# Four edits to the first attention stage of a four-stage Trainium2 kernel: V's low half by TensorE and ScalarE, the layer norm's last step on ScalarE, the bias on GpSimd, the output tile by blocks

## The chip, the cores and the metric

The kernel runs on one core of one Trainium2 chip. The metric is device time in microseconds (us) of one launch, the median of several runs. The engines are named as the profile names them: PE (TensorE, matmuls), PEld (TensorE's weight loads), DVE (VectorE), ACT (ScalarE), POOL (GpSimd) and SP (SyncE, which issues most of the DMAs). Each engine works through its own list in order, and semaphores tie the lists together.

## The reference

Four layers follow one another on an input of 8 batches of 512 tokens of width 128: attention with relative positions (16 heads of size 64), a top-2 mixture of experts, a second attention, and a mixture of experts with capacity. Behind each stands a residual sum and a layer norm without learned scale. The change touches the first layer alone. Cut to it:

```python
def _layernorm(x, axis=-1, eps=1e-05):
    m = jnp.mean(x, axis=axis, keepdims=True)
    v = jnp.var(x, axis=axis, keepdims=True)
    return (x - m) / jnp.sqrt(v + eps)
...
        w = qkv * (3.0 * x * h * n) ** (-0.25)
        q, k, v = jnp.einsum('bsx,xAnh->Abnsh', input, w)
        q = q + q_bias[:, None, :]
        a = jnp.einsum('bnqh,bnkh->bnqk', q, k) * h ** (-0.5)
...
        a = a + relative_causal(pos_scores)
        mask = jnp.tril(jnp.ones((s, s), dtype=bool))
        a = jax.nn.softmax(jnp.where(mask, a, NEG_INF), axis=-1)
        o = jnp.einsum('bnqk,bnkh->bqnh', a, v).reshape(b, s, n * h)
        fan_in, fan_out = out_kernel.shape
        out = o @ (out_kernel * (fan_in * fan_out) ** (-0.25)) + out_bias
        return out
```

The first layer's result is the layer norm of `input + out`.

## The kernel before

The first attention is `rel_attention_phase`. It takes the profile's stretch from about 35 us to 763 us. Its unit of work is a **pair** of heads of one batch: 8 pairs (`PAIRS`) by 8 batches (`B`), numbered `n`, with `p` the pair in its batch and `k` the parity of a double buffer. `schedule` writes the same loop on every engine: it calls `body(n, t, b, p, k)` once for each pair. The order of `body` on an engine is the order of its list. Nothing reorders it.

Products run in float16 halves: each operand is split into a high half and the rest, and three matmuls take the place of one. Who makes the halves:

- **POOL**, `split_k` and `split_q`: four splits in a pair (K and Q of head 0, then of head 1), each an affine select that writes the high half (L705) and a subtraction for the low half (L708). They are made for pair n+1 while pair n is worked on. `split_k(0, n+1)` waits for ACT's `k_copy`. PE's `scores(h, n+1)` (L483 to L486) wait for the splits of head h.
- **The probabilities**: ACT's `exps` (L565) and `high` (L574), then DVE's `low` (L618), which reads the 128x1280 probabilities and their high half, both in SBUF. SP transposes both halves by DMA.
- **V**: PE's `project_v` writes V to the PSUM tile `v_ps`. ACT's `v_high` (L580) copies it to the float16 tile `v_h`. DVE's `v_low` (L637) writes the rest, `v_l`.

DVE's `body` for a pair is: `maxima` of head 0 (L606), `reciprocals` and `low` of head 1 of the pair before, `q_evac` (L624), `reciprocals` (L614), `normalise` of the pair two before (L632), `low` of head 0, `maxima` of head 1, `q_evac` of the next pair, `v_low`. ACT's is: three groups of `exps` with `k_copy` (L586) between, `high`, `v_high`, then `exps` and `high` of head 1. PE's is: scores of head 0, projections of K and Q of head 0 of the next pair and V of this one, `weighted_values` (L502) of the pair two before, scores of head 1, projection of Q of head 1, and `project_out` (L519) of the pair two before, which uses the tile `o32` as weights. `o32` has the query index outside and the block index c inside, so that a block's weights are every fourth float32.

Once in a batch more is done. At the last pair (`wrap`) DVE adds the output bias to this batch's rows of `m.x` (`add_bias`, L642) and applies the layer norm of the batch before (`batch_norm`, the helper at L123: subtract the mean, multiply by the inverse deviation, four instructions). At the third pair (p = 2) DVE sums output and residual and takes the statistics of the batch before, and POOL makes the inverse deviation (`layer_norm_gpsimd`, L136 and L137).

## Time and profile before

| | us |
|---|---|
| median of three runs | 1621.62 |
| lowest and highest run | 1618.57, 1624.36 |
| the profiled execution | 1622.89 |
| its span | 1621.2 |
| PE busy in the span | 1395.3 (86%) |
| DVE busy | 1300.4 (80%) |
| ACT busy | 944.1 (58%) |
| POOL busy | 886.5 (55%) |

Shares of busy time run over all four stages. In the first stage DVE, PE and POOL each show nine or eight tenths in most slices, so that a share alone doesn't tell which one sets the pace. What tells it is the idle time in front of an instruction and the engine that ended it. A row of the view in order of time gives the start in us from the span's start, the duration in us, the engine, the line, the operation, the tiles written and read, and in brackets the idle time before it with what ended it.

### The profile page before, as it was taken

The page shows a single profiled execution, that of the slowest core. Times are in us where ns is not written, and L with a number is a line of the kernel's source. Part 1 is how long each engine was busy: PE and PEld are TensorE (multiplying, and loading weights), DVE is VectorE, ACT ScalarE, POOL GpSimd, SP SyncE. Part 2 cuts the span into 40 slices and gives each one's busy share as a digit, 9 for nine tenths or more (in the row PEclk, how much of TensorE's full clock was granted, in tenths as well). Part 3 has the DMA queues.
Part 4 walks back from the last instruction along what each step waited for, and adds up shares of the span by engine and source line. Part 5 has one row for each costly group of instructions (what it writes and reads, how often), then busy time and mean ns, then how long its engine had stood idle before and what let it go on. Part 6 is the DMA issues. An engine that isn't in the chain of part 4 may idle for free. (4 is left out here: it accounts for less than half of the span.)

```text
span 1621.2 us, 36711 instructions
## 1 busy us (share of the span) xinstructions
PE 1395.3 (86%) x11495; PEld 838.3 (52%) x11495; DVE 1300.4 (80%) x2722; ACT 944.1 (58%) x1857; POOL 886.5 (55%) x943
## 2 busy tenths in 40 slices
PE   4799999999999999995798987489899899997936
PEld 3477767676776767674465664123333332332316
DVE  3689899999899999996688888377787887887834
ACT  2577767776767777673244443156666666665631
POOL 2678878888888878785355555211221231231635
PEclk9799999999999999997699999599999999999978
DMA  5667766665666656663000000421011111101001
GB/s 161 123 144 156 142 147 142 145 150 137 152 140 151 145 138 150 143 146 85 1 1 0 0 0 16 138 50 34 28 39 33 32 33 31 39 27 32 26 8 33
DMA packets 401552, 133.51 MB, mean 82 GB/s; under 512 B 362155, under 2 KB 389792, under 8 KB 401376
## 3 DMA queue, kind: packets, MB, share of 16 engines
q1 hardware_dynamic: 398144, 128.41, 33.7%
q10 hardware_dynamic: 1824, 3.15, 0.6%
q0 software_dynamic: 1536, 1.34, 0.3%
q8 instruction: 26, 0.43, 0.1%
q14 instruction: 22, 0.18, 0.0%
HBM read 37.14 MB, written 13.15 MB: 31 GB/s over the span
## 5 line engine op out<-in xcount | busy, mean ns | idle before, releaser
L565 ACT ACTIVATE prob<-score_ps,nmax 128x512 f32<-128x512 f32 (+3 forms) x512 | 264.1, 524 | 194.5 <-DVE nmax L606 193.9
L1577 DVE TENSOR_REDUCE a_nm<-a_s 128x1 f16<-128x512 f32 x512 | 324.5, 687 | 53.1 <-PE a_s L1349 52.1
L1503 ACT ACTIVATE a_pt<-a_st 128x1024 f32<-128x1024 f32 x256 | 260.5, 1021 | 122.0 <-PE a_st L1367 118.8
L1349 PE MATMUL a_s<-a_kop,a_qop 128*128 128x512 f16 x512 | 198.2, 388 | 59.1 <-DVE a_nm L1577 42.3
L606 DVE TENSOR_REDUCE nmax<-score_ps 128x1 f32<-128x512 f32 (+3 forms) x512 | 219.3, 480 | 19.6 <-PE score_ps L486 17.2
L618 DVE SCALAR_TENSOR_TENSOR p<-prob,p 128x1280 f16<-128x1280 f32 x128 | 224.6, 1755 | 3.4 <-ACT p L574 3.3
L708 POOL TENSOR_TENSOR q_l<-q,q_h 128x512 f16<-128x512 f32 x130 | 202.3, 1556 | 10.8
L483 PE MATMUL score_ps<-k_h,q_h 128*128 128x512 f16 (+3 forms) x512 | 158.2, 309 | 37.2 <-POOL q_l L708 31.2
L574 ACT ACTIVATE p<-prob 128x1280 f16<-128x1280 f32 x128 | 162.6, 1270 | 8.4
L708 POOL TENSOR_TENSOR k_l<-k,k_h 64x512 f16<-64x512 f32 x130 | 157.8, 1214 | 10.8
L902 ACT ACTIVATE hid<-fps,b_cols 128x512 f32<-128x512 f32 x130 | 86.4, 687 | 126.6 <-PE fps L862 126.6
L485 PE MATMUL score_ps<-k_h,q_l 128*128 128x512 f16 (+3 forms) x512 | 157.2, 307 | 0.0
L484 PE MATMUL score_ps<-k_l,q_h 128*128 128x512 f16 (+3 forms) x512 | 157.1, 307 | 0.0
L998 POOL TENSOR_TENSOR hid_l<-hid,hid_h 128x512 f16<-128x512 f32 x65 | 97.1, 1494 | 106.4 <-DVE hid_h L966 106.4
L1367 PE MATMUL a_st<-a_qop,a_kop 128*128 128x512 f16 x512 | 152.2, 380 | 0.2
L1349 PEld LDWEIGHTS a_s<-a_kop,a_qop 128*128 128x128 f16 x512 | 50.5, 99 | 184.7 <-DVE a_nm L1577 151.6
L705 POOL TENSOR_SCALAR_AFFINE_SELECT q_h<-q 128x512 f16<-128x512 f32 x130 | 122.9, 945 | 39.7 <-POOL k_l L708 34.4
L1380 PE MATMUL a_pv<-a_pt,a_vaug 128*32 128x512 f32 x1024 | 137.0, 607 | 0.7 <-ACT a_pt L1503 0.7
L519 PEld LDWEIGHTS out_ps<-wo,o 128*128 128x128 f32 x512 | 124.3, 327 | 18.6 <-DVE o L632 12.1
L519 PE MATMUL out_ps<-wo,o 128*128 128x128 f32 (+1 forms) x512 | 125.2, 389 | 9.2 <-DVE o L632 9.2
L705 POOL TENSOR_SCALAR_AFFINE_SELECT k_h<-k 64x512 f16<-64x512 f32 x130 | 84.0, 646 | 84.6 <-ACT k L586 68.5
L502 PE MATMUL pv_ps<-pt,v_h 128*64 128x256 f16 (+1 forms) x1536 | 119.1, 259 | 2.2 <-DMA pt<-p 2.2
(328 smaller groups left out, 3216.6 us busy)
## 6 DMA issues: line engine op xcount, KB each, us to landing
r_bc<-r_parts SPq DMA_DIRECT2D x128, 128.0 KB, 2.9
a_qop<-q_parts SPq DMA_DIRECT2D x32, 128.0 KB
a_kop<-k_parts SPq DMA_DIRECT2D x128, 24.0 KB
x_tok<-in_L_attn_input_dram SPq DMA_DIRECT2D x4, 512.0 KB, 12.4
pt<-p SPq DMA_TRANSPOSE x128, 4.1
r_parts<-rsum SPq DMA_DIRECT2D x128, 2.0 KB, 2.1
e_w<-in_L_ffn_w_dram SPq DMA_DIRECT2D x1, 2048.0 KB, 8.8
q_parts<-a_q_h SPq DMA_DIRECT2D x16, 128.0 KB
```

What stands on the lines that cost most here:

```text
L483: nc.tensor.matmul(o, q_h[h][:, qs], m.k_h[h][:, 0:w], start=True, stop=False)
L485: nc.tensor.matmul(o, q_l[h][:, qs], m.k_h[h][:, 0:w], start=False, stop=False)
L519: mm = nc.tensor.matmul(out_ps[:, cs], o32[:, :, c], w, start=False, stop=(end and c == QC - 1), skip_group_check=True)
L565: ins = nc.scalar.activation(prob[h][:, P_OFF[c]:P_OFF[c] + w], score_ps[u][:, col:col + w], ACT.Exp, bias=nmax[h][:, c:c + 1], accum_out= ...
L574: nc.scalar.activation(p16[h][k][:, 0, :], prob[h][:, :], ACT.Copy, scale=P_SCALE).then_inc(p_hi[h], 1)
L606: ins = nc.vector.tensor_reduce(nmax[h][:, c:c + 1], score_ps[u][:, col:col + P * (c + 1)], AX.X, ALU.max, negate=True)
L618: nc.vector.scalar_tensor_tensor(p16[h][k][:, 1, :], prob[h][:, :], P_SCALE, p16[h][k][:, 0, :], ALU.mult, ALU.subtract).then_inc(p_lo[h], 1)
L705: nc.gpsimd.affine_select(out=hi, in_=src, compare_op=ALU.is_ge, fill=0.0, base=0, pattern=[[1, S]], channel_multiplier=0).then_inc(pool_s ...
L708: return nc.gpsimd.tensor_tensor(lo, src, hi, ALU.subtract)
L1349: nc.tensor.matmul(s_ps[k][:, :], qop[:, g, c * P:(c + 1) * P], kop[:, hh, g, :], start=True, stop=True).then_inc(s_mm[k], 1)
L1503: nc.scalar.activation(pt[kc % 2][r][:, :, :], st_ps[r][:, :, :], ACT.Exp, scale=1.0 / SC).then_inc(exp_done[r], 1)
L1577: nc.vector.tensor_reduce(nm[g % 2][:, c, hh:hh + 1], s_ps[c % 2][:, :], AX.X, ALU.max, negate=True).then_inc(max_done[c % 2], 1)
```

## The change

Four things move, and some semaphores with them.

1. **V's low half.** V is kept in PSUM without its scale, and its halves are made of V/32. ACT copies V/32 to `v_h`. A new PE matmul (`take_high`, behind the scores of head 1) adds `v_h` times minus 32 to `v_ps`, through the new tile `take` (a scaled identity), which leaves V less its high half. A new ACT copy (`v_low`, behind `v_high`) takes that to `v_l`. DVE's `v_low` goes. The missing scale stands in the factor of `batch_sum`.
2. **The layer norm's last step** becomes an ACT instruction with a bias and a scale from pointers, four for each batch, behind `high` of head 1 of the last pair. POOL makes the minus mean and its product with the inverse deviation (`norm_terms`): four small instructions in place of two.
3. **The output bias** is added by POOL, four instructions of 128x128, behind the splits of the second pair (p = 1).
4. **`o32`** is laid out by blocks: PE's weights are 128 neighbouring float32, and DVE writes with a step of 128 elements.

Also: the semaphores `r_done` and `f0_loaded` go, SP's `store_r` waits for `p_lo` in place of `r_done` (in its list the same semaphore value has been waited for just ahead), PE waits once at the start for `take`, and the later stages wait for one counter of all weight loads.

```diff
...
 P_SCALE = 1024.0
+V_SCALE = 1.0 / 32
...
         r_bc = [sb(f"r_bc{k}", [P, S], F32) for k in range(2)]
-        o32 = sb("o32", [P, P, QC], F32)
+        o32 = sb("o32", [P, S], F32)
...
         rstd = sb("ln_rstd", [P, QC], F32)
+        take = sb("take_away", [P, P], F16)
+        nmean, shift = sb("ln_nmean", [P, QC], F32), sb("ln_shift", [P, QC], F32)
...
         k_mm, k_out, k_split = sem("k_mm"), sem("k_out"), pair("k_split")
-        v_mm, v_hi, v_lo = sem("v_mm"), sem("v_hi"), sem("v_lo")
+        v_mm, v_hi, v_rest, v_lo = sem("v_mm"), sem("v_hi"), sem("v_rest"), sem("v_lo")
...
         s_mm, max_done, exp_done = pair("s_mm"), pair("max_done"), pair("exp_done")
-        p_hi, p_lo, r_done = pair("p_hi"), pair("p_lo"), pair("r_done")
+        p_hi, p_lo = pair("p_hi"), pair("p_lo")
...
-                sp.wait_ge(r_done[h], n + 1)
+                sp.wait_ge(p_lo[h], n + 1)
...
                     o = v_ps[:, c * P:(c + 1) * P]
-                    nc.tensor.matmul(o, x_hi, w_hi, start=True, stop=False)
-                    nc.tensor.matmul(o, x_hi, w_lo, start=False, stop=False)
-                    mm = nc.tensor.matmul(o, x_lo, w_hi, start=False, stop=True)
+                    nc.tensor.matmul(o, x_hi, w_hi, start=(c == 0), stop=False, skip_group_check=True)
+                    nc.tensor.matmul(o, x_hi, w_lo, start=False, stop=False, skip_group_check=True)
+                    mm = nc.tensor.matmul(o, x_lo, w_hi, start=False, stop=False, skip_group_check=True)
...
+            def take_high(n, k):
...
+                pe.wait_ge(v_hi, n + 1)
+                nc.tensor.matmul(v_ps[:, :], take[:, :], v_h[k][:, :, :].rearrange("p c n -> p (c n)"), start=False, stop=True,
+                                 skip_group_check=True).then_inc(v_rest, 1)
...
                     cs = slice(c * P, (c + 1) * P)
-                    mm = nc.tensor.matmul(out_ps[:, cs], o32[:, :, c], w, start=False, stop=(end and c == QC - 1), skip_group_check=True)
+                    mm = nc.tensor.matmul(out_ps[:, cs], o32[:, cs], w, start=False, stop=(end and c == QC - 1), skip_group_check=True)
...
             def first_front():
+                pe.wait_ge(bias_in, 1)
...
                 scores(1, n)
+                take_high(n, k)
...
                 nc.scalar.activation(v_h[k][:, :, :].rearrange("p c n -> p (c n)"), v_ps[:, :], ACT.Copy,
-                                     scale=W_SCALE).then_inc(v_hi, 1)
+                                     scale=V_SCALE).then_inc(v_hi, 1)
...
+            def v_low(n, k):
+                act.wait_ge(v_rest, n + 1)
+                nc.scalar.activation(v_l[k][:, :, :].rearrange("p c n -> p (c n)"), v_ps[:, :], ACT.Copy,
+                                     scale=V_SCALE).then_inc(v_lo, 1)
...
+            def batch_norm(b):
+                act.wait_ge(m.rstd_ready, b + 1)
+                for c in range(QC):
+                    ins = nc.scalar.activation(m_flat(m.x)[:, ds(b * S + c * D, D)], y[:, c, :], ACT.Identity,
+                                               bias=shift[:, c:c + 1], scale=rstd[:, c:c + 1])
+                ins.then_inc(ln_dve, 1)
...
                 v_high(n, k)
+                v_low(n, k)
...
                 high(1, n, t, k)
+                if at(p, PAIRS - 1) and not at(b, 0):
+                    batch_norm(b - 1)
...
             nc.scalar.preload_act_table(ACT.Exp)
-            schedule(act, lambda: k_copy(0), body, lambda: None)
+            schedule(act, lambda: k_copy(0), body, lambda: batch_norm(B - 1))
...
                     dve.wait_ge(r_stored, 32 * (n - 1))
-                nc.vector.reciprocal(rsum[h][k][:, :], sums[h][:, :]).then_inc(r_done[h], 1)
+                nc.vector.reciprocal(rsum[h][k][:, :], sums[h][:, :])
...
                     dve.wait_ge(out_mm, n)
-                nc.vector.tensor_tensor(o32[:, :, :], pv_ps[:, :].rearrange("p (c q) -> p q c", q=P),
+                nc.vector.tensor_tensor(o32[:, :].rearrange("p (c q) -> p q c", q=P), pv_ps[:, :].rearrange("p (c q) -> p q c", q=P),
...
-
-            def v_low(n, k):
-                dve.wait_ge(v_hi, n + 1)
-                nc.vector.scalar_tensor_tensor(v_l[k][:, :, :].rearrange("p c n -> p (c n)"), v_ps[:, :], W_SCALE,
-                                               v_h[k][:, :, :].rearrange("p c n -> p (c n)"), ALU.mult, ALU.subtract).then_inc(v_lo, 1)
...
-
-            def add_bias(b):
-                xb = m_flat(m.x)[:, ds(b * S, S)].rearrange("p (c d) -> p c d", d=D)
-                nc.vector.tensor_tensor(xb, xb, m.bo_bc[:, :].unsqueeze(1).to_broadcast([P, QC, D]), ALU.add).then_inc(bias_in, 1)
...
                 dve.wait_ge(out_mm, PAIRS * (b + 1))
-                dve.wait_ge(bias_in, b + 1)
+                dve.wait_ge(bias_in, b + 2)
...
                 dve.wait_ge(ln_dve, b + 1)
-                nc.vector.scalar_tensor_tensor(y[:, :, :].rearrange("p c d -> p (c d)"), out_ps[:, :], O_SCALE / P_SCALE,
+                nc.vector.scalar_tensor_tensor(y[:, :, :].rearrange("p c d -> p (c d)"), out_ps[:, :], O_SCALE * W_SCALE / (P_SCALE * V_SCALE),
...
-            def batch_norm(b):
-                layer_norm_apply(nc, dve, m, b, y, mv, rstd,
-                                 m_flat(m.x)[:, ds(b * S, S)].rearrange("p (c d) -> p c d", d=D)).then_inc(ln_dve, 1)
...
                 wrap = at(p, PAIRS - 1)
-                behind = wrap and not at(b, 0)
...
                 q_evac(1, n + 1, pw)
-                v_low(n, k)
-                if wrap:
-                    add_bias(b)
-                if behind:
-                    batch_norm(b - 1)
...
                 vector_gate(nc, m).then_inc(ln_dve, 1)
+                nc.vector.tensor_scalar(take[:, :], m.ident[:, :], -1.0 / V_SCALE, None, ALU.mult).then_inc(bias_in, 1)
...
                 batch_stats(B - 1)
-                batch_norm(B - 1)
...
                 split_q(1, n + 1)
+                if at(p, 1):
+                    add_bias(b)
                 if at(p, 2) and not at(b, 0):
-                    layer_norm_gpsimd(nc, pool, m, b - 1, mv, ve, rstd)
+                    norm_terms(b - 1)
+            def add_bias(b):
+                for c in range(QC):
+                    xc = m_flat(m.x)[:, ds(b * S + c * D, D)]
+                    ins = nc.gpsimd.tensor_tensor(xc, xc, m.bo_bc[:, :], ALU.add)
+                ins.then_inc(bias_in, 1)
+            def norm_terms(b):
+                steps = Steps(pool, m.ln_pool, 2 * b)
+                pool.wait_ge(m.var_ready, b + 1)
+                nc.gpsimd.tensor_tensor(nmean[:, :], mv[:, :, 0], m.minus[:, :], ALU.mult)
+                steps.step(nc.gpsimd.tensor_tensor(ve[:, :], mv[:, :, 1], m.eps[:, :], ALU.add))
+                steps.step(nc.gpsimd.tensor_tensor(rstd[:, :], ve[:, :], m.mhalf[:, :], ALU.pow))
+                nc.gpsimd.tensor_tensor(shift[:, :], nmean[:, :], rstd[:, :], ALU.mult).then_inc(m.rstd_ready, 1)
```

What stands in a row on DVE at the end of a batch's last pair and in front of the next batch, before:

```order
L632 TENSOR_TENSOR o<-pv_ps,r_bc 128x512
L618 SCALAR_TENSOR_TENSOR p_01<-prob,p_01 128x1280
L606 TENSOR_REDUCE nmax<-score_ps 128x1 x4
L624 SCALAR_TENSOR_TENSOR q_1<-q_ps,q_bias,q_mult 128x512
L637 SCALAR_TENSOR_TENSOR v_l<-v_ps,v_h 128x512
L642 ISA
L642 TENSOR_TENSOR x_tok<-x_tok,bo_bc 128x512
L123 TENSOR_SCALAR x_tok<-ln_y,ln_mv,ln_rstd 128x128
```

And there now:

```order
L640 RECIPROCAL rsum<-sums 128x4
L658 TENSOR_TENSOR o<-pv_ps,r_bc 128x128x4
L644 SCALAR_TENSOR_TENSOR p_01<-prob,p_01 128x1280
L632 TENSOR_REDUCE nmax<-score_ps 128x1 x4
L650 SCALAR_TENSOR_TENSOR q_1<-q_ps,q_bias,q_mult 128x512
L357 REGISTER_ALU
L357 COMPARE_AND_BRANCH
L640 RECIPROCAL rsum<-sums 128x4
```

`v_low`, the bias and the four steps of the layer norm (the first of them is the last row of the first piece) are gone from DVE.

On POOL, the end of a batch's second pair (in all batches but the first), before:

```order
L708 TENSOR_TENSOR k_l<-k,k_h 64x512
L705 AFFINE_SELECT q_h<-q_1 128x512
L707 REGISTER_ALU
L708 TENSOR_TENSOR q_l<-q_1,q_h 128x512
L719 REGISTER_ALU
L720 REGISTER_ALU
```

Now:

```order
L715 TENSOR_TENSOR k_l<-k,k_h 64x512
L712 AFFINE_SELECT q_h<-q_1 128x512
L714 REGISTER_ALU
L715 TENSOR_TENSOR q_l<-q_1,q_h 128x512
L750 ISA
L750 TENSOR_TENSOR x_tok<-x_tok,bo_bc 128x128
L750 ISA
L750 TENSOR_TENSOR x_tok<-x_tok,bo_bc 128x128
```

The row pairs at L750 come four times, and the next pair's splits start behind them.

On ACT, from `v_high` of a batch's last pair on, now (`p_11` and `prob` are head 1's probabilities):

```order
L590 REGISTER_ALU
L591 ACTIVATE v_h<-v_ps 128x512
L596 ACTIVATE v_l<-v_ps 128x512
L576 ACTIVATE prob,sums<-score_ps,nmax 128x512
L576 ACTIVATE prob,sums<-score_ps,nmax 128x384
L576 ACTIVATE prob,sums<-score_ps,nmax 128x128
L576 ACTIVATE prob,sums<-score_ps,nmax 128x256
L585 ACTIVATE p_11<-prob 128x1280
L602 ISA
L602 ACTIVATE x_tok<-ln_y,ln_shift,ln_rstd 128x128
L602 ISA
```

The second copy of V (L596) is new behind the first (L591), and the layer norm (L602, four times) stands ahead of the next batch's first exponentials.

## Rows read from the trace of the kernel before

**Rows 1.** Busy time by engine between K copies: stretch, length, PE, PEld, DVE, ACT, POOL.

```profile
473.01:486.70 13.69, 12.93 (x143) 9.74 (x140) 12.95 (x22) 7.80 (x22) 9.72 (x9) 1.00 0.49 116
486.70:496.32 9.62, 8.11 (x59) 5.53 (x57) 9.32 (x17) 7.69 (x22) 7.73 (x8) 1.00 0.67 158
...
549.64:560.01 10.37, 10.04 (x99) 7.55 (x97) 9.57 (x17) 7.69 (x22) 9.20 (x9) 1.00 0.67 151
sum 87.00, PE 82.07 PEld 61.00 DVE 81.25 ACT 61.96 POOL 73.68; mean PE 10.26 PEld 7.62 DVE 10.16 ACT 7.75 POOL 9.21
```

**Rows 2.** POOL in order of time, one ordinary pair.

```profile
466.38 1.56 POOL L705 TENSOR_SCALAR_AFFINE_SELECT q_h<-q 128x512 f16<-128x512 f32 x1 [0.26 <-POOL k_l L708]
468.02 1.16 POOL L708 TENSOR_TENSOR q_l<-q,q_h 128x512 f16<-128x512 f32 x1
...
472.14 2.43 POOL L708 TENSOR_TENSOR q_l<-q,q_h 128x512 f16<-128x512 f32 x1
```

**Rows 3.** DVE in order of time, the same pair.

```profile
464.67 0.69 DVE L632 TENSOR_TENSOR o<-pv_ps,r_bc 128x512 f32<-128x512 f32 x1 [0.67 <-PE pv_ps L502]
465.28 2.19 DVE L618 SCALAR_TENSOR_TENSOR p<-prob,p 128x1280 f16<-128x1280 f32 x1
...
469.64 0.68 DVE L637 SCALAR_TENSOR_TENSOR v_l<-v_ps,v_h 128x512 f16<-128x512 f32 x1
470.24 1.85 DVE L606 TENSOR_REDUCE nmax<-score_ps 128x1 f32<-128x512 f32 x4
...
472.09 1.46 DVE L618 SCALAR_TENSOR_TENSOR p<-prob,p 128x1280 f16<-128x1280 f32 x1
```

**Rows 4.** PE in order of time: output projection, next scores; transposes in the second stage.

```profile
477.52 1.92 PE L519 MATMUL out_ps<-wo,o 128*128 128x128 f32 x8
479.77 0.39 PE L483 MATMUL score_ps<-k_h,q_h 128*128 128x512 f16 x1 [0.33 <-POOL q_l L708]
...
766.82 1.97 PE L826 MATMUL fps<-ident,x_tok 128*128 128x128 f32 x8 [2.49 <-DVE wg_l L918]
```

**Rows 5.** DVE in order of time, the last pair of a batch.

```profile
480.69 1.50 DVE L642 TENSOR_TENSOR x_tok<-x_tok,bo_bc 128x512 f32 x1
482.11 2.39 DVE L123 TENSOR_SCALAR x_tok<-ln_y,ln_mv,ln_rstd 128x128 f32 x4
484.41 1.67 DVE L606 TENSOR_REDUCE nmax<-score_ps 128x1 f32<-128x512 f32 x4
```

**Rows 6.** ACT in order of time, the same place.

```profile
478.55 0.69 ACT L565 ACTIVATE prob<-score_ps,nmax 128x512 f32<-128x512 f32 x1 [2.61 <-DVE nmax L606]
...
480.73 1.27 ACT L574 ACTIVATE p<-prob 128x1280 f16<-128x1280 f32 x1
485.13 0.69 ACT L565 ACTIVATE prob<-score_ps,nmax 128x512 f32<-128x512 f32 x1 [3.13 <-DVE nmax L606]
...
486.36 0.36 ACT L565 ACTIVATE prob<-score_ps,nmax 128x128 f32<-128x128 f32 x1
486.70 0.60 ACT L586 ACTIVATE k<-k_ps 128x512 f32<-128x512 f32 x1
```

**Rows 7.** POOL in order of time: behind the wrap, then the next batch's third pair.

```profile
487.58 0.60 POOL L705 TENSOR_SCALAR_AFFINE_SELECT k_h<-k 64x512 f16<-64x512 f32 x1 [3.69 <-ACT k L586]
...
507.56 1.23 POOL L705 TENSOR_SCALAR_AFFINE_SELECT k_h<-k 64x512 f16<-64x512 f32 x1 [0.59 <-ACT k L586]
...
517.42 1.45 POOL L136 TENSOR_TENSOR ln_ve<-ln_mv,ln_eps 128x4 f32<-128x4 f32 x1
```

**Rows 8.** POOL groups over the whole span: count, busy us, mean ns.

```profile
L1699 POOL TENSOR_TENSOR a_vaug<-a_v,a_bv 128x128 f32<-128x128 f32 x32 | 14.4, 454 | 184.0 <-PE a_pv L1380 129.7 <-DVE a_v L1552 54.3
L1743 POOL TENSOR_TENSOR a_scale<-a_mv,a_rstd 128x4 f32<-128x4 f32 x8 | 1.6, 202 | 0.6
```

**Rows 9.** Weight load groups over the whole span: weights in steps of four, weights side by side.

```profile
L519 PEld LDWEIGHTS out_ps<-wo,o 128*128 128x128 f32 x512 | 124.3, 327 | 18.6 <-DVE o L632 12.1
L826 PEld LDWEIGHTS fps<-ident,x_tok 128*128 128x128 f32 x32 | 5.9, 218 | 7.8 <-issue 5.2 <-DVE wg_l L918 2.6
```

More of the change, by code:

```diff
@@ L133, in layer_norm_gpsimd @@
 def layer_norm_gpsimd(nc, pool, m, n, mv, ve, rstd):
-    steps = Steps(pool, m.ln_pool, n)
+    steps = Steps(pool, m.ln_pool, n + B)
     pool.wait_ge(m.var_ready, n + 1)
@@ L271, in _ @@
             nc.gpsimd.memset(m.eps[:, :], LN_EPS)
+            nc.gpsimd.memset(m.minus[:, :], -1.0)
             nc.gpsimd.memset(m.b2_blocks[:, :], 0.0)
@@ L364, in _ @@
         def _(sp):
-            load = lambda dst, src: sp.dma_start(dst, src).then_inc(m.f0_loaded, 16)
+            load = lambda dst, src: sp.dma_start(dst, src).then_inc(m.a_loaded, 16)
             load(m.w1_raw[:, :, :], io["L0_ffn_W1"].rearrange("e d f -> d e f"))
@@ L373, in _ @@
             load(m.iota8[:, :], io["c_iota8"])
-            loads = 0
+            loads = 10 * 16
             def load(dst, src, scattered=False):
@@ L442, in _ @@
             schedule(sp, lambda: None, body, last)
-            sp.wait_ge(m.f0_loaded, m.F0_LOADS)
             sp.wait_ge(m.a_loaded, loads)
@@ L734, in body @@
                 split_q(1, n + 1)
+                if at(p, 1):
+                    add_bias(b)
                 if at(p, 2) and not at(b, 0):
-                    layer_norm_gpsimd(nc, pool, m, b - 1, mv, ve, rstd)
+                    norm_terms(b - 1)
[11 more added lines that the diff above has]
+                nc.gpsimd.tensor_tensor(shift[:, :], nmean[:, :], rstd[:, :], ALU.mult).then_inc(m.rstd_ready, 1)
             def last():
-                layer_norm_gpsimd(nc, pool, m, B - 1, mv, ve, rstd)
+                norm_terms(B - 1)
             schedule(pool, lambda: front(0), body, last)
@@ L828, in _ @@
                 if t == 0:
-                    pe.wait_ge(m.f0_loaded, m.F0_LOADS)
+                    pe.wait_ge(m.a_loaded, m.A_LOADS)
                     nc.tensor.transpose(hid_ps[0][:, 0:E0 * FC], m.b1_rows[:, :], m.ident[0:E0 * FC, 0:E0 * FC]).then_inc(b1_mm, 1)
@@ L914, in _ @@
             steps = Steps(dve, dsteps)
-            dve.wait_ge(m.f0_loaded, m.F0_LOADS)
+            dve.wait_ge(m.a_loaded, m.A_LOADS)
             nc.vector.tensor_copy(wg_h[:, :], m.wg_raw[:, :]).then_inc(wg_split, 1)
@@ L998, in low @@
                 nc.gpsimd.tensor_tensor(hid_l[k][1][:, :], hid32[k][1][:, :], hid_h[k][1][:, :], ALU.subtract).then_inc(h_lo[1], 1)
-            pool.wait_ge(m.f0_loaded, m.F0_LOADS)
+            pool.wait_ge(m.a_loaded, m.A_LOADS)
             for hi, raw in ((w1_h, m.w1_raw), (w2_h, m.w2_raw)):
@@ L1961, in build @@
         m.eps = sb("ln_eps", [P, QC], F32)
+        m.minus = sb("ln_minus", [P, QC], F32)
         m.gate_v = sb("gate_v", [P, 1], F32)
@@ L1974, in build @@
         m.iota8 = sb("iota8", [P, E0], F32)
-        m.f0_loaded = ctx.enter_context(nc.semaphore("f0_loaded"))
-        m.F0_LOADS = 10 * 16
         m.a_w = sb("a_w_raw", [P, 5, D], F32)
```

## The prediction, made before the changed kernel was run

> **What bounds the kernel now.** All four edits lie in the first attention, so I read that stage alone, first by stretches. Busy time between two K copies of ACT gives the length of each pair: eight pairs, one batch, take 87.0 us, an ordinary one 10.37, the last of a batch 13.69, the one behind it 9.62 [rows 1]. Then I read each engine in order of time, for what it waits for.
>
> In an ordinary pair POOL waits for nobody. Its four splits follow one another with 0.26 us or less between, and they are longer than their work: an affine select (0.60 in rows 7) once takes 1.56, a subtraction of 1.16 once takes 2.43 [rows 2]. Both times DVE's `low` is running: `low` of head 0 is asked for at 465.28, waits until the K subtraction ends at 466.12 (0.26 us before 466.38), and holds the select that starts at 466.38; `low` of head 1 starts at 472.09, 0.05 us ahead of the subtraction at 472.14 [rows 2, 3]. So POOL's splits plus 0.95 and 1.27 us of such stalls make up 10.4 us, and that is the pair. PE is nearly as full: its output projection ends at 479.44 and the next scores start at 479.77, where POOL's low half of Q releases them [rows 4]. DVE has 0.67 us in front of `normalise` [rows 3], ACT 2.61 us in front of its exponentials of head 1 [rows 6]. **POOL sets an ordinary pair.** The Trainium skill, "SBUF — State Buffer", section "SBUF: two separate sides", says the same of the port that VectorE and GpSimd share: it is locked for a whole instruction by a GpSimd operation or by a VectorE one with two SBUF inputs. By that rule `v_low`, with one input in PSUM, takes nothing from POOL, and the trace agrees: it has its 0.68 us in rows 3.
>
> At a batch's end the bound is another one. DVE does the bias (1.42 us to the next start) and the layer norm (2.30) before it comes to the maxima at 484.41 [rows 5]; ACT waits 3.13 us for them, and the K copy comes at 486.70 [rows 6]; POOL waits 3.69 us for that copy [rows 7]. **There DVE sets the time.**
>
> **V's low half.** DVE loses 0.60 us (469.64 to 470.24) in each of 64 pairs [rows 3]. The maxima behind it read scores that PE started 0.14 us after POOL's subtraction ended at 469.18 [rows 2, 4]; the first unit takes PE some 0.92, which gives 470.24. The maxima would start when they start now, so I count 0. If POOL were no bound, the whole 0.60 would count. PE gains one matmul with 512 columns, whose kind takes 0.39 in rows 4 and less to the next start. The 0.33 us in front of the scores covers it [rows 4]. Its wait for `v_h` holds up only the Q projection and the output projection; the copy is done before the scores of head 1 end. ACT gains a copy of 0.60 (as the K copy [rows 6]), which waits for that matmul. The hole of 2.61 us holds the wait and the copy: scores of head 1 end near 476.9, the matmul near 477.3, the copy near 477.9, and the exponentials start at 478.55. I take 0; the bounds are -0.6 and +0.4 for each pair.
>
> **The wrap.** Bias and layer norm leave DVE, so the maxima start near 480.7 instead of 484.41. ACT then ends `high` of head 1 at 481.9 (start 480.73 and 1.18 to the next) and does the layer norm itself. No row shows this instruction. The nearest is the exponential of 128 columns, 0.36, or 0.34 to the next start [rows 6]; its input is in PSUM and it has one pointer. I take 0.38 each, 1.5 for four, bounds 1.2 and 1.9. The next exponentials then start at 483.4 instead of 485.13: **-1.7 for a wrap**, and not the 3.7 that DVE loses. POOL's hole of 3.69 mostly closes: `low` of head 1 now comes near 482.5, stalls the subtraction there by 1.27, and POOL ends near 485.0, still ahead of the K copy. Six wraps make -10.2. The last one has no maxima and exponentials behind it: `low` stands right behind the layer norm, which by rows 5 is the time 484.41, and now waits only for its own high half (481.9) and the end of a split, some 0.3 later: -2.2. The first has the bias alone, and there the same stall of POOL takes the gain back: -0.2. Sum -12.6.
>
> **Bias on POOL.** Four instructions of 128x128: 0.45 each [rows 8], with an address instruction between that the trace shows as 0.07 or so elsewhere, or 0.41 each if they overlap as neighbours do: 1.65 to 2.1. They are put behind the splits of the second pair. POOL has a hole there, 0.59 in front of the split at 507.56, but that split ends only at 508.79, since `low` holds it until 508.2 [rows 7]; the hole hides nothing. Behind the four, `low` of head 0 now meets the K splits instead of the subtraction of Q, so the scores come 1.7 to 2.4 later. POOL carries this to the next batch's wrap, for it has no other hole.
>
> **The small terms.** `norm_terms` has two instructions of 0.20 more, one behind a wait: +0.45 in each batch [rows 8]. The first of the four takes the stall that makes 1.45 of the first one now [rows 7]. With the bias I count 2.6 for a batch (bounds 1.6 and 3.4), seven batches, **+18.2**. In the first batch POOL has holes of several us and the term is 0. At the end of the stage the norm is on the path: 0.3 for POOL, 0.4 for ACT against DVE; and 0.3 for the wait for `take` at the start: +1.0.
>
> **`o32` by blocks.** A weight load takes 327 ns in steps of four and 218 side by side [rows 9]. Yet eight output matmuls take 1.92 and eight with neighbouring weights 1.97 [rows 4]: the loads run under the matmuls, and the gain is 0 to 0.1 for a pair, where PE has 0.33 to spare: 0. DVE now writes at a step of 512 bytes, which no row shows. Bounds: 0 (reading PSUM at that step costs nothing seen: 0.69 for 512 columns in rows 3) and, by the 109 ns that 128 weights lose in rows 9, four times that, 0.44. In an ordinary pair `normalise` may end 0.8 us later before `low` is later, since `low` waits for the K subtraction anyway [rows 2, 3]. I take 0. The Trainium skill, same page, section on the DMA port swizzle, speaks against this edit: it says that accesses which each cross to a new 16-byte line pay a penalty. By the weight loads the trace agrees; by the same price DVE would lose 0.44, the second rival's term.
>
> **Sum.** -12.6 + 18.2 + 1.0 = +6.6 us against the profiled execution's 1622.9 (span 1621.2, 1.7 around it). The median is 1.3 below it, so the forecast is 1621.6 + 6.6 = **1628 us**, 0.4% slower.
>
> **The rivals.**
> 1. *POOL takes the new work in its holes.* If the bias falls where POOL waits for the K copy, or the order of the locks turns once in a batch so that a stall of 1.27 goes, a batch costs 1.3 less: -9, 1619. For it speaks that the margin is 0.05 us [rows 2, 3]; against it that POOL has no hole in six pairs of eight. If both happen, 2.6 a batch go and the wraps alone count: 1610. 25% and 8%.
> 2. *The strided write is on DVE's path.* At 0.44 or more, `low` of head 0 in the pairs where DVE has no slack (the first and third of a batch) starts behind the next POOL instruction and loses up to 1.2 more: 1 us for each of 15 pairs, +13 with the new stalls, 1641. It decides from 0.8 us of extra write in an ordinary pair: then all 64 lose. 17%.
> 3. *The order of locks turns in every pair.* If PE's new matmul delays the scores by more than 0.05 us, the subtraction goes ahead of `low`, POOL gains about 0.5 a pair: -28, 1595. Against it: PE has 0.33 to spare [rows 4]. 5%.
> 4. *The edit does nothing:* `o32` is such a case already, in the sum with 0. That the DVE instructions go is seen in the order of the lists.
>
> **How the numbers follow.** Forecast 1628, its own spread 1621 to 1635: 45%. Rival 1: 33%, rival 2: 17%, rival 3: 5%. A difference of 0.3%, 4.9 us, is about what a measurement of this kernel can tell from none: below 1616.7 is faster, above 1626.5 slower. Faster: rival 3, the 8% and a little of the rest, 0.22. Slower: rival 2 and 60% of the forecast, 0.44. Same: 0.34. The range leaves out rival 3 and the tails: 1608 to 1642.
>
> **What would show it.** Right: ordinary pairs stay at 10.4, DVE idle before the maxima of head 0 where `v_low` was; the wrap falls to about 12; POOL's hole there falls below 1; the third pair of a batch grows by 2 us or more. Wrong: ordinary pairs shorter than 10.2 (DVE was the bound, or the locks turned), `normalise` longer than 0.7 us, ACT's norm instruction above 0.5 us, or the third pair unchanged, which would say that POOL had room.

## The result: 0.7% slower

| | before | changed |
|---|---|---|
| median, us (five runs each) | 1624.31 | 1635.96 |
| lowest and highest | 1618.57, 1624.56 | 1632.54, 1638.00 |
| the profiled execution | 1622.89 | 1635.96 |
| its span | 1621.2 | 1634.2 |

The ratio of changed to before is 1.0073, with a 95% interval of 1.0059 to 1.0088. The forecast was 1628 us, some 6.6 us slower; the spans differ by 13.0. The direction was right, the size was half of it.

Where the 13.0 us come from, by the starts of ACT's K copies: the first one comes 1.2 us later (38.0 for 36.9), from there to the last it is 11.5 us more (708.6 for 697.1), and from the last to the end of the program 0.4 more. In that last part the first stage ends 1.2 us earlier, and the stages that weren't changed take 1.6 more. That 1.6 can't be put down to the edits: over all traces of this document those stages take between 857.7 and 860.9 us.

The same batch as in [rows 1], now: busy time of each engine between K copies of ACT. Columns: stretch, length, busy time of PE, PEld, DVE, ACT and POOL with the count of instructions, granted TensorE clock, DMA share, GB/s.

```profile
480.60:492.58 11.98, 10.99 (x131) 8.25 (x130) 10.05 (x17) 9.82 (x27) 10.80 (x9) 1.00 0.70 143
492.58:502.17 9.59, 8.17 (x74) 5.49 (x70) 7.86 (x14) 8.25 (x23) 7.74 (x8) 1.00 0.75 146
502.17:512.52 10.35, 9.46 (x102) 6.82 (x99) 9.12 (x17) 8.27 (x23) 9.18 (x9) 1.00 0.76 158
512.52:524.40 11.88, 9.61 (x101) 6.87 (x99) 11.26 (x25) 8.29 (x23) 10.87 (x13) 1.00 0.65 133
524.40:537.15 12.75, 10.04 (x90) 6.84 (x87) 8.70 (x16) 8.62 (x24) 11.37 (x13) 0.87 0.65 134
537.15:549.00 11.85, 10.92 (x113) 7.65 (x111) 10.12 (x16) 8.40 (x22) 8.03 (x8) 1.00 0.61 120
549.00:558.85 9.85, 9.37 (x101) 6.79 (x98) 8.61 (x16) 8.29 (x24) 7.96 (x8) 1.00 0.80 163
558.85:569.23 10.38, 9.41 (x100) 6.77 (x98) 9.07 (x16) 8.30 (x24) 9.21 (x9) 1.00 0.77 152
```

Before, the eight pairs took 13.69, 9.62, 10.37, 11.09, 10.65, 10.76, 10.45 and 10.37. The wrap (first row) has lost 1.7 us. The fourth to sixth have gained 0.8, 2.1 and 1.1, the seventh lost 0.6. In the fifth row the clock is 0.87, in all others 1.00. This is so in every batch from the second to the eighth (once a 0.99 stands behind the 0.87). Before, the clock is below 1.00 in one pair of the second, third and fifth batch (0.83 to 0.86), and in none of the other four.

By batch, the lengths are:

| batch | 1 | 2 | 3 | 4 | 5 | 6 | 7 | 8 |
|---|---|---|---|---|---|---|---|---|
| before | 88.7 | 85.4 | 87.4 | 87.0 | 87.6 | 87.0 | 87.0 | 87.0 |
| changed | 88.3 | 88.2 | 88.7 | 88.7 | 88.7 | 88.7 | 88.8 | 88.7 |

POOL of the changed kernel in order of time: the bias (L750), and the first and last of the layer norm's four small instructions.

```profile
512.76 2.95 POOL L750 TENSOR_TENSOR x_tok<-x_tok,bo_bc 128x128 f32 x4
...
525.90 0.20 POOL L757 TENSOR_TENSOR ln_nmean<-ln_mv,ln_minus 128x4 f32<-128x4 f32 x1
...
527.43 1.50 POOL L760 TENSOR_TENSOR ln_shift<-ln_nmean,ln_rstd 128x4 f32<-128x4 f32 x1
```

The bias takes 2.91 us to the next start. DVE's `low` runs from 512.11 to 514.15 meanwhile and holds the port. The four small ones take 2.98 us up to the start of the select that follows, where two took 2.50 before; the last of them stands under a `low` again (1.50 for 0.20).

PE of the changed kernel, from the output projection (L528) of the third pair on, L492 the first scores of a pair, L456 to L458 the projection of K:

```profile
517.37 1.05 PE L528 MATMUL out_ps<-wo,o 128*128 128x128 f32 x8
520.69 0.39 PE L492 MATMUL score_ps<-k_h,q_h 128*128 128x512 f16 x1 [2.27 <-POOL q_l L715]
520.92 0.38 PE L493 MATMUL score_ps<-k_l,q_h 128*128 128x512 f16 x1
...
532.88 0.39 PE L492 MATMUL score_ps<-k_h,q_h 128*128 128x512 f16 x1 [2.71 <-POOL q_l L715]
...
536.05 0.63 PE L457 MATMUL k_ps<-xt_h,w_l 128*128 x1
536.48 0.63 PE L458 MATMUL k_ps<-xt_l,w_h 128*128 x1
```

Two things stand here that the prediction doesn't have. The eight output matmuls (the trace shows two for each of the four calls) take 1.05 us in place of the 1.92 of [rows 4]. And PE waits 2.27 and then 2.71 us for POOL, where it waited 0.46 (for ACT) and 1.01 before. Soon behind the second wait the clock falls from the higher to the lower of its levels: from 533.75 to about 537.2 matmuls of 512 columns come 0.43 us apart (536.05 and 536.48) in place of 0.22 or so (520.69 and 520.92). The K copy waits for that. It comes 4.27 us behind the first scores (537.15 and 532.88); in e4_filler below, where the clock is held, it comes 3.39 behind them, so that the fall makes it 0.9 us late.

### The profile page after: what moved, and what is told of

Same layout as the page of the kernel before. It is cut to its first block and busy times, and to the rows that moved or that the text cites. A ratio compares the mean times of both kernels' runs of the same rounds, so it can differ in the third digit from the quotient of the medians.

```text
span 1634.2 us, 36942 instructions
## 1 busy us (share of the span) xinstructions
PE 1357.1 (83%) x11559; PEld 791.3 (48%) x11559; DVE 1252.3 (77%) x2619; ACT 993.2 (61%) x1953; POOL 907.8 (56%) x992
## 3 DMA queue, kind: packets, MB, share of 16 engines
q1 hardware_dynamic: 398144, 128.41, 36.9%
## 5 line engine op out<-in xcount | busy, mean ns | idle before, releaser
L492 PE MATMUL score_ps<-k_h,q_h 128*128 128x512 f16 (+3 forms) x512 | 158.0, 309 | 82.9 <-POOL q_l L715 73.5
L644 DVE SCALAR_TENSOR_TENSOR p<-prob,p 128x1280 f16<-128x1280 f32 x128 | 215.0, 1680 | 3.9 <-ACT p L585 3.4
L715 POOL TENSOR_TENSOR q_l<-q,q_h 128x512 f16<-128x512 f32 x130 | 201.5, 1550 | 10.8
L715 POOL TENSOR_TENSOR k_l<-k,k_h 64x512 f16<-64x512 f32 x130 | 152.4, 1172 | 10.8
L712 POOL TENSOR_SCALAR_AFFINE_SELECT k_h<-k 64x512 f16<-64x512 f32 x130 | 85.4, 657 | 74.6 <-ACT k L609 58.4
L1723 POOL TENSOR_TENSOR a_vaug<-a_v,a_bv 128x128 f32<-128x128 f32 x32 | 14.4, 453 | 184.1 <-PE a_pv L1404 129.8
L495 PE MATMUL score_ps<-causal,ident_bf 128*128 128x128 bf16 x512 | 114.8, 224 | 0.0
```

The costliest lines, as they stand in the source:

```text
L492: nc.tensor.matmul(o, q_h[h][:, qs], m.k_h[h][:, 0:w], start=True, stop=False)
L644: nc.vector.scalar_tensor_tensor(p16[h][k][:, 1, :], prob[h][:, :], P_SCALE, p16[h][k][:, 0, :], ALU.mult, ALU.subtract).then_inc(p_lo[h], 1)
L712: nc.gpsimd.affine_select(out=hi, in_=src, compare_op=ALU.is_ge, fill=0.0, base=0, pattern=[[1, S]], channel_multiplier=0).then_inc(pool_s ...
L715: return nc.gpsimd.tensor_tensor(lo, src, hi, ALU.subtract)
```

## Experiments

All times below are medians of 6 to 12 runs beside 23 to 35 runs of the kernel before on the same chip; before stood at 1622.9, 1621.5 and 1622.4 us in the three groups. A batch's length is taken from the K copies of the profiled execution. A steady batch is one from the third to the eighth.

### One edit undone

The changed kernel with the bias on DVE, the layer norm on DVE, or the old `o32`:

```diff
 # e1_bias_dve: POOL's add_bias goes; DVE, behind q_evac(1, n + 1, pw):
+                if wrap:
+                    add_bias(b)
 # e2_norm_dve: ACT's batch_norm and POOL's norm_terms go; DVE, same place:
+                if wrap and not at(b, 0):
+                    batch_norm(b - 1)
 # e3_o32_old; the weights of project_out and the write of normalise follow
-        o32 = sb("o32", [P, S], F32)
+        o32 = sb("o32", [P, P, QC], F32)
```

> The changed kernel with one edit undone: the output bias is added by DVE behind the last pair's second q_evac again, in one instruction. Theory A (the bias on POOL is what costs: the three pairs behind it grew by 0.8, 2.1 and 1.0 us against the kernel before, and one got 0.6 shorter): a batch falls from 88.7 to 85.7 to 86.5 us, seven batches give back 15 to 21 us, time 1615 to 1621, below the kernel before (ratio 0.995). The wrap stays within 0.5 us of 11.98, since 1.42 us of bias on DVE lie beside ACT's 1.6 us of layer norm. Theory B (the wider write of o32 or the new copies of V cost in every pair): nothing changes, 1632 to 1638.

Measured: 1620.91 us, ratio 0.999 (0.9978 to 1.0002). Steady batches take 86.0 to 87.6, the wrap 11.98. That is theory A's time at its upper edge: the ratio falls from 1.0073 to 0.999, which is some 13 us and less than the 15 to 21 expected. The bias on DVE costs the wrap nothing beside ACT's layer norm. It doesn't follow that the bias alone made the kernel slow, for the third run below gives back nearly as much without touching it.

> The changed kernel with the layer norm's last step on DVE again, and POOL with its two instructions for the inverse deviation in place of four. Theory A: at the wrap DVE does 2.3 us more and ACT 1.6 less, so the wrap grows by 0.2 to 0.7 us; POOL loses 0.2 to 1.5 us a batch in the fourth pair (its last small instruction stands under a lock of low for 1.5). Sum -1 to +0.3 a batch: 1628 to 1638, ratio 1.003 to 1.009. Rival: the layer norm on ACT is worth its whole 1.7 us a wrap, 1645 or more.

Measured: 1627.04, ratio 1.0026 (1.0016 to 1.0037), better than both expected. The wrap is 11.77, so ACT's layer norm brings nothing there once the bias is off DVE. Without the two small instructions PE waits 2.1 in place of 2.7 us in the fourth pair, and the clock falls there in four of the last six batches: those take 87.9 to 88.2, the other two 86.5 and 86.7.

> The changed kernel with o32 laid out as before. normalise falls from 1.06 to 0.69 us, eight output matmuls rise from 1.05 to 1.92 us. Theory A (POOL sets ordinary pairs): ordinary pairs stay at 10.37, since PE keeps some 0.1 us ahead of the scores; the stretches in which PE waits long for scores are shorter by 0 to 0.9: 1633 to 1638. Theory B (the wide write stands on DVE's path): -13, 1621 to 1625. Theory C (the faster projection is what keeps PE off the path, with V's extra matmul): PE's 1.92 and 0.22 more fill its slack of 0.33, pairs grow by 0.1 to 0.3, 1640 to 1650.

Measured: 1623.97, ratio 1.0005 (0.9993 to 1.0017). This is theory B's number, some 11 us back by the ratios, where theory A had 3 at most. Yet ordinary pairs stay at 10.37, so B's mechanism, a cost in every pair, is wrong. The clock still falls in five of the last seven batches. DVE, POOL and the stretches around such a fall, with the old layout (L658 `normalise`, L644 `low`, L715 the subtraction of Q):

```profile
429.80:442.70 12.90, 11.34 (x92) 7.99 (x90) 8.11 (x16) 8.50 (x23) 11.10 (x13) 0.87 0.63 132
442.70:453.20 10.50, 10.50 (x104) 7.95 (x103) 8.45 (x16) 8.43 (x23) 8.17 (x8) 1.00 0.70 138
```

```profile
445.49 0.69 DVE L658 TENSOR_TENSOR o<-pv_ps,r_bc 128x512 f32<-128x512 f32 x1 [1.10 <-PE pv_ps L511]
446.09 1.55 DVE L644 SCALAR_TENSOR_TENSOR p<-prob,p 128x1280 f16<-128x1280 f32 x1
```

```profile
446.38 2.27 POOL L715 TENSOR_TENSOR q_l<-q,q_h 128x512 f16<-128x512 f32 x1
```

And the same place in the changed kernel:

```profile
540.35 1.06 DVE L658 TENSOR_TENSOR o<-pv_ps,r_bc 128x512 f32<-128x512 f32 x1 [1.32 <-PE pv_ps L511]
541.25 2.19 DVE L644 SCALAR_TENSOR_TENSOR p<-prob,p 128x1280 f16<-128x1280 f32 x1
```

```profile
540.95 1.16 POOL L715 TENSOR_TENSOR q_l<-q,q_h 128x512 f16<-128x512 f32 x1
```

With the old layout `low` comes 0.29 us ahead of the subtraction and the pair takes 10.50. With the new one `normalise` is 0.3 us longer, `low` comes 0.30 us behind the subtraction, takes 2.19, and the pair takes 11.85. The write is half of this shift: `normalise` also starts 0.29 us nearer to the subtraction (0.60 ahead for 0.89). So the layout helps to turn an order of locks here, in the pair behind a fall of the clock. In f2_o32_only below the write alone turns it.

### The clock held up

```diff
                     project_out(n - 2, ...)
+                if at(p, 2) or not isinstance(p, int):
+                    for _ in range(8 if at(p, 2) else 4):
+                        nc.tensor.matmul(out_ps[:, :], m.zeros[:, 0:P], m.zeros[:, :], start=False, stop=False, ...)
```

> The changed kernel with work added to PE alone: zeros are added to out_ps, eight matmuls of 512 columns behind the output projection of the third pair of each batch and four in each of the four pairs behind it (0.22 us each, 1.8 and 0.9 us, into stretches in which PE waits 2.3, 2.7 and 0.9 us). Theory C2 (half of the extra cost is TensorE's clock: behind two waits of 2.3 and 2.7 us the granted clock of one pair is 0.87 and its matmuls take 0.63 in place of 0.38 for some 3.5 us): with PE kept busy the clock stays at 1.00, that pair and the next lose 1 to 2.5 us, seven batches 7 to 17 us: 1619 to 1629. Theory A alone (POOL sets the pace there too): 1633 to 1638. If the added matmuls cost by themselves: above 1640.

Measured: 1628.29, ratio 1.0038 (1.0025 to 1.0051). Work was added, and the time fell: by the ratios some 6 us, by the profiled spans 6.8 (1627.4 for 1634.2). The second row is the stretch that had 0.87:

```profile
508.10:519.98 11.88, 11.34 (x109) 7.56 (x107) 11.26 (x25) 8.30 (x23) 10.87 (x13) 1.00 0.65 132
519.98:531.84 11.86, 10.01 (x101) 6.83 (x98) 8.38 (x16) 8.53 (x24) 10.69 (x13) 1.00 0.71 144
531.84:542.60 10.76, 10.65 (x111) 7.46 (x109) 9.35 (x16) 8.40 (x24) 9.59 (x9) 1.00 0.69 133
542.60:553.05 10.45, 10.42 (x108) 7.23 (x104) 9.21 (x16) 8.30 (x24) 9.28 (x9) 1.00 0.74 151
```

From the third batch on the clock is 1.00 in all pairs; 12.75 + 11.85 + 9.85 have become 11.86 + 10.76 + 10.45, and the batch 87.3 (88.1 in the third). POOL's and DVE's lists are those of the changed kernel. So of the 1.7 us that most batches grew by, the fall of the clock with what follows from it makes 1.4. PE still waits 1.85 us in the stretch that had 0.87.

### One edit alone

Each is the changed kernel with the other three undone.

> Only the first edit is left of the four: V's low half by PE and ACT. Bias and layer norm are on DVE at the wrap, o32 is laid out as before. Theory A (POOL sets an ordinary pair): ordinary pairs stay at 10.37 to 10.45; the wrap, which DVE sets, gets 0.6 us shorter (13.69 to 13.1), 7 wraps make -4: 1616 to 1622, ratio 0.996 to 1.000. Rival: PE's extra matmul takes the slack of 0.33 us in front of the scores and turns the order of the locks, then pairs change by 0.1 or more, that is 6 us or more either way.

Measured: 1619.35, ratio 0.9989 (0.9980 to 0.9998). Ordinary pairs are unchanged to 0.1 us, the wrap is 13.35, 0.33 shorter, and a batch 86.6.

> Only the layer norm's last step is moved to ACT, with its four small instructions on POOL. DVE leaves 2.3 us at the wrap, ACT's exponentials start behind its layer norm: the wrap falls from 13.69 to 12.0 to 12.3. POOL's two further instructions cost 0.2 to 1.2 us a batch. Sum -1.6 to -0.3 a batch: 1611 to 1620, ratio 0.993 to 0.998. If the layer norm on ACT is worth nothing, 1622 or more.

Measured: 1619.02, ratio 0.9982 (0.9970 to 0.9993). The wrap is 11.98, a steady batch 85.9 to 86.8; in three of the last six the clock falls in one pair.

> Only the bias is moved to POOL, in its place behind the splits of the second pair. The wrap gets 1.4 us shorter (12.3), the pairs behind the four instructions together 2.2 to 3.3 longer: +0.8 to +1.9 a batch, 1628 to 1636. Theory D: PE's waits there are shorter than in the changed kernel (its output projection takes 1.92 us), so that the granted clock stays at 1.00 in most batches and the lower end is right; if the clock falls here as well, the upper.

Measured: 1632.95, ratio 1.0065 (1.0053 to 1.0077), the upper end. The wrap is 13.02, only 0.7 shorter. In five of the last six batches the clock falls in two pairs, to 0.83 and 0.86, and they take 88.5 to 88.9; in the last it doesn't fall, and that takes 87.9. So the bias's own cost is 0.9 us a batch, 1.6 in the pairs behind the wrap less 0.7 at the wrap.

> Only the layout of o32 is changed, all else as in the kernel before. Theory D (the layout costs nothing by itself, but lengthens PE's waits and so lets the clock fall where POOL is late): without the bias on POOL PE's longest waits of a batch are near 2 us, and ordinary pairs stay at 10.37; with no pair below a clock of 1.00 in the steady batches 1620 to 1626, with one such pair a batch 1630 to 1634. Theory B (normalise, 0.37 us longer, stands on DVE's path in every pair): 64 times 0.3, 1640 or more.

Measured: 1633.58, ratio 1.0069 (1.0049 to 1.0088). The layout alone costs as much as all four edits. From the third batch on each takes 88.8 or 88.9, and the clock is 0.87 in the fourth stretch. Theory D gave the number. What it left out is where a part of PE's wait comes from. The third pair, DVE (L635 `normalise`, L621 `low`), then POOL (L710) and PE:

```profile
515.27 1.03 DVE L635 TENSOR_TENSOR o<-pv_ps,r_bc 128x512 f32<-128x512 f32 x1
516.15 2.45 DVE L621 SCALAR_TENSOR_TENSOR p<-prob,p 128x1280 f16<-128x1280 f32 x1
```

```profile
516.10 1.16 POOL L710 TENSOR_TENSOR q_l<-q,q_h 128x512 f16<-128x512 f32 x1
```

```profile
520.07 0.39 PE L486 MATMUL score_ps<-k_h,q_h 128*128 128x512 f16 x1 [2.55 <-ACT prob L568]
```

In the kernel before, the same two engines in the same place:

```profile
510.16 0.66 DVE L632 TENSOR_TENSOR o<-pv_ps,r_bc 128x512 f32<-128x512 f32 x1
510.74 1.50 DVE L618 SCALAR_TENSOR_TENSOR p<-prob,p 128x1280 f16<-128x1280 f32 x1
```

```profile
510.98 2.27 POOL L708 TENSOR_TENSOR q_l<-q,q_h 128x512 f16<-128x512 f32 x1
```

Before, `low` is asked for 0.24 us ahead of the subtraction. Now `normalise` is 0.30 longer, `low` comes 0.05 behind it and takes 2.45 for 1.50. The maxima are 1.25 us later, ACT and the scores with them. PE has done its output projection 0.84 us sooner. The two add up to the 2.09 us by which PE's wait has grown, from 0.46 to 2.55, and no run parts them. Then the clock falls: matmuls take the longer time from 520.5 to 523.9.

The same filler as above in this kernel:

> The layout of o32 changed alone, as one run before (88.8 us a batch, one pair at a granted clock of 0.87), and zeros added to out_ps by PE behind the output projection: eight matmuls of 0.22 us in the third pair, four in each of the next four. Theory D (of the 1.8 us a batch that the layout costs, one part is that low of head 0 comes behind POOL's subtraction in the third pair, 0.95 us, and the other the clock that falls behind PE's wait of 2.55 us): the clock stays at 1.00, a batch falls to 87.2 to 87.9 us, 1624 to 1629, between the two kernels. If the wide write costs by itself and not the clock: 1632 to 1636.

Measured: 1631.59, ratio 1.0051 (1.0035 to 1.0067), slower than expected. The clock is held where the filler stands, but in four batches it falls two pairs earlier, where there is none. First the third pair of the fifth batch, where the clock is held, and the pair behind it; then a stretch where it falls:

```profile
423.69:436.04 12.35, 11.49 (x110) 7.42 (x106) 12.31 (x26) 7.70 (x22) 10.20 (x11) 1.00 0.65 130
436.04:445.98 9.94, 9.94 (x103) 7.05 (x101) 9.21 (x17) 7.70 (x22) 8.93 (x9) 1.00 0.80 158
```

```profile
490.83:501.49 10.66, 8.32 (x50) 4.76 (x49) 9.34 (x17) 7.93 (x23) 8.02 (x8) 0.84 0.70 141
```

The fifth and eighth batch have the clock at 1.00 throughout: both take 87.2, for 88.8 without filler and 87.0 in the kernel before. The other four of the steady ones take 87.5 to 88.4. That some 1.6 of the 1.8 us hang on the clock is read from two batches, then, and not from the median.

In these two batches the order of locks is turned all the same (L638 `normalise`, L624 `low`, L713 the subtraction):

```profile
427.13 1.03 DVE L638 TENSOR_TENSOR o<-pv_ps,r_bc 128x512 f32<-128x512 f32 x1
428.01 2.45 DVE L624 SCALAR_TENSOR_TENSOR p<-prob,p 128x1280 f16<-128x1280 f32 x1
```

```profile
427.95 1.16 POOL L713 TENSOR_TENSOR q_l<-q,q_h 128x512 f16<-128x512 f32 x1
```

The pair takes 12.35 for 11.09, but the next two take 9.94 and 10.37 for 10.65 and 10.76, so that all but 0.2 us comes back. With the clock held, the turned order costs next to nothing.

### Versions built on this

The bias needs no time of POOL, and of DVE only once, in the first pair, to make its two halves: PE opens `out_ps` with a matmul of zeros anyway.

```diff
 # g1_bias_pe: the changed kernel, POOL's add_bias goes, PE's open_output:
-                nc.tensor.matmul(out_ps[:, :], m.zeros[:, 0:P], m.zeros[:, :], start=True, stop=False, ...)
+                for i, t in enumerate((bo_h, bo_l)):
+                    nc.tensor.matmul(out_ps[:, :], ones[:, :], t[:, :, :].rearrange(...), start=(i == 0), stop=False, ...)
 # g2_norm_early: g1, and in ACT's body the layer norm stands here
                 v_high(n, k)
+                if at(p, PAIRS - 1) and not at(b, 0):
+                    batch_norm(b - 1)
                 v_low(n, k)
 # g3_best: g2 with o32 as in the kernel before
```

> The changed kernel without a bias on POOL or DVE: PE's matmul of zeros that opens out_ps is replaced by two that add the bias (its high and low half, scaled, times a tile of ones). Theory A: POOL loses the whole of its 3 us there, PE gains 0.22, nothing comes to DVE: a batch takes 86.0 us or a little less, as with the bias on DVE under ACT's layer norm, 1617 to 1622. If a pair of each batch still falls to a clock of 0.87: 1624 to 1630.

Measured: 1621.93, ratio 0.9995 (0.9981 to 1.0009); a steady batch 86.2, or 87.0 and 87.6 in the two with a fall.

> As the kernel with the bias from PE, and ACT's layer norm stands between its two copies of V, where ACT waits 1.3 us for PE, in place of behind the high half of head 1. Expected: the wrap falls from 12.0 to 10.4 to 11.0 us, since POOL's splits then set it as in any other pair; 7 wraps, -7 to -11 us: 1609 to 1615. If the delay of V's low half (0.3 us) or of the exponentials of head 1 is on the path, -3 us only.

Measured: 1614.25, ratio 0.9954 (0.9939 to 0.9969). The wrap is an ordinary pair now. Its stretch, and ACT there (L597 and L602 the two copies of V, L608 the layer norm):

```profile
470.60:481.06 10.46, 9.47 (x102) 6.83 (x100) 9.14 (x16) 9.72 (x27) 9.29 (x9) 1.00 0.74 150
```

```profile
472.96 0.58 ACT L597 ACTIVATE v_h<-v_ps 128x512 f16<-128x512 f32 x1
473.44 1.64 ACT L608 ACTIVATE x_tok<-ln_y,ln_shift,ln_rstd 128x128 f32 x4
474.98 0.58 ACT L602 ACTIVATE v_l<-v_ps 128x512 f16<-128x512 f32 x1
```

The four steps of the layer norm fill the time in which ACT waited for `take_high`. This version is faster than both kernels (0.5% below the one before). Its trace also has both orders of locks at one clock. In the third pair of the sixth batch `low` is the one that waits (2.44 us, the subtraction 1.16); this pair and the next two take 12.36, 10.53 and 10.37, the batch 85.4. In the fifth batch the subtraction waits (2.54, `low` 1.48); the three take 11.38, 11.27 and 10.77, the batch 85.5. In both the two instructions start within 0.06 us of each other, `low` second, so that at such a margin only the durations tell who got the lock.

> As the kernel before it (bias from PE, layer norm between the copies of V), and o32 laid out as in the kernel before. Theory D: low of head 0 stands ahead of POOL's subtraction in the third pair again and PE's waits get shorter; 0.8 to 1.5 us a batch: 1604 to 1611, ratio to the kernel before 0.989 to 0.994. If PE is the bound by now, its slower output projection costs: above 1612.

Measured: 1614.05, ratio 0.9948 (0.9928 to 0.9967). The old layout adds nothing that can be told from the version ahead of it, and the expected 1604 to 1611 was wrong: the layout's cost depends on what else stands in those pairs, and here the clock falls once in each of the last three batches all the same (85.2 to 85.7 with and 85.2 to 85.3 without).

## The prediction, point by point

**The direction is in part luck.** The forecast had the kernel slower by what POOL gets, less what the wrap gains, with `o32` at nothing. The kernel that fits this sum is e3_o32_old, and it isn't slower: 1.0005 (0.9993 to 1.0017) for the 1.004 forecast. The changed kernel's slowdown needs `o32`, which stood in the sum with 0, and the clock, which didn't stand there.

**POOL sets an ordinary pair: right.** The third stretch of a steady batch, which has no extra work on POOL, stays at 10.37 in the changed kernel and in nearly all batches of the other versions that have no fall of the clock ahead of it, although `v_low` is gone from DVE and PE's list got 0.6 us shorter.

**V's low half, counted at 0: right in the pairs.** Alone it gives -0.33 at the wrap. ACT's second copy waits 1.2 to 1.5 us for PE in most pairs, 0.5 behind the wrap, in the hole that was named for it.

**The wrap, -1.7: right** (13.69 to 11.98). ACT's layer norm takes 1.54 us to the next start, 0.38 each, as taken. But the reading that it stands on the path was worth more than the forecast made of it: moved by a few lines, 1.5 us more go at each wrap.

**Bias and small terms on POOL, +2.6 a batch: the pairs behind the wrap are 3.3 longer**, within the bounds (1.6 to 3.4), but for another reason, for all four edits are in this number. With the clock held (e4_filler) they are only 2.0 longer, and with the old `o32` (e3_o32_old) 1.7 to 2.3. Alone and without a fall, the bias makes them 1.6 longer (last batch of f4_bias_only) and the small terms 0.6 (fourth batch of f3_norm_only). So POOL's own share was put somewhat too high, and the clock's share of 1.4 is missing from the sum altogether. The bias itself takes 2.9 and not 1.65 to 2.1, because a `low` stands over its first instruction; the small terms' own time grew by 0.48, as forecast (0.45). For the batches from the second on the forecast has +7.8 us and the traces +11.9: these 4 us are the greater part of the 6.4 between forecast and measured spans, and 1.6 more lie in the stages that weren't changed.

**`o32`, counted at 0: the step that failed.** It went wrong twice. For PE it said "the loads run under the matmuls, and the gain is 0 to 0.1", since eight transposes with neighbouring weights took 1.97 in [rows 4]. Another kind of instruction was taken as the measure: the projection itself now takes 1.05, 0.87 less. The weight loads in [rows 9] were the better row. They now read:

```profile
L528 PEld LDWEIGHTS out_ps<-wo,o 128*128 128x128 f32 x512 | 67.8, 194 | 18.5 <-DVE o L658 9.7
```

For DVE the write costs 0.30, inside the bounds of 0 and 0.44, but "I take 0" overlooked what 0.3 us can turn. The second rival had this mechanism, `low` behind POOL's next instruction, and its place, "the first and third of a batch"; the rows of f2_o32_only show it in the third. Its threshold was put at 0.44 where 0.30 sufficed: the margin was the 0.24 us between 510.74 and 510.98, and those two rows stood in the trace of before. Its price, 1 us for each such pair, was wrong too: the following pairs give it back where the clock holds (h1_o32_filler). What costs is PE's wait, which both halves of this edit lengthen, and the fall of the clock behind it.

**The small ends.** The start was put at +0.3: the first K copy comes 1.2 later, but the first batch gives 0.3 back. The end was put at -1.5 net and gave -1.2.

**What the signs were worth.** The wrap near 12, POOL's hole there below 1 (0.85) and unchanged ordinary pairs came as said; ACT's norm instruction took 0.48, just below the 0.5 that would have spoken against. The third pair was to grow by 2 us or more and grew by 0.8; the 2.1 came in the fourth, where the clock falls. "`normalise` longer than 0.7 us" was named as a sign against the forecast, and came (1.06). A fall of the clock was not on the list. The third rival's -28 was counted from the kernel before, the changes of the other two from the forecast.

**Still open.** Why the clock falls in one batch and not in the next with nearly the same waits (e2_norm_dve, e3_o32_old, h1_o32_filler). What a fall costs isn't one number either: 1.4 in the changed kernel, 0.4 to 0.6 in the kernel before (87.4 and 87.6 for 87.0), 0.8 in e3_o32_old where it comes in the fourth pair and 0 to 0.2 where it comes in the third, 0 to 0.5 in g3_best. And how the costs share out: alone the layout costs 0.69% and the bias 0.65%, the other two gain 0.11% and 0.18%; the sum is 1.05%, and all four together cost 0.73%, a gap hardly beyond the intervals. From the other side it is plain: undoing the bias gives back 0.83% and undoing the layout 0.68%, together twice what there is. The two dear ones spend the same thing, PE's waits in the third and fourth pair. That is an argument from the rows and not a measured split.

## What to carry to other kernels

Where one engine waits for another at every turn, look at the start of each two-input DVE instruction against the GpSimd instruction next to it: an order of locks with 0.2 us of margin can turn, and then moves about 1 us from one pair to another. Follow it through the next pairs before it goes into the sum, for here it came back, and what it left was a longer wait of TensorE. An engine made faster off the critical path waits longer too, and on TensorE a longer wait can cost the clock; work put on the engine that already sets the pace makes such waits. Before a step is moved to another engine, ask whether a matmul that is issued anyway can carry it, and put what remains in a hole of its new engine, not behind its last instruction.

## What the runs showed of the hardware

- **The clock of TensorE falls to its lower level behind some of PE's waits of 1.3 to 2.9 us** in these kernels, not behind all of them (not behind the 2.27 shown above; in h1_o32_filler behind a wait of 2.10 in four batches and not in two), and stays there for some 3.5 us (matmuls of 512 columns 0.43 us apart for 0.22). Adding 0.9 to 1.8 us of matmuls into the waits kept it at 1.00 in that place and made the program some 6 us faster.
- **Float32 weights side by side** make eight 128x128 matmuls take 1.05 us in place of 1.92, and their loads 194 ns in place of 327.
- **A DVE write at a step of 512 bytes** of 128x512 float32 from PSUM takes 1.06 us for 0.69.
- **The lock between DVE and POOL.** The Trainium skill, "SBUF — State Buffer", section "SBUF: two separate sides", states that VectorE and GpSimd lock each other out of their shared port and that the one which starts first holds it for its whole instruction. Here the trace agrees at each of the places shown: `low` 0.29 us ahead gives 1.55 for it and 2.27 for the subtraction, 0.30 us behind gives 2.19 and 1.16.
- **Four GpSimd additions of 128x128** take 2.95 us where the first stands under such a lock (1.71) and 1.68 where none does, in the first batch; one alone takes 0.45.
- **A ScalarE instruction of 128x128** with a bias and a scale from pointers, SBUF to SBUF, takes 0.48 us, or 0.38 to the next.
